# Layer 2 of a two-layer transformer block: four gathers of batch 1 in front of batch 0's root on GpSimd, batch 2's gathers behind batch 1's root, and bounds on three register loads

## The reference

```python
def reference(x, ctx_2048, _lenS2, g_xattn, g_ffn, ...):
    x = x + jnp.tanh(g_xattn[0]) * _L0_xattn_ref(_layernorm(x, axis=-1), ctx_2048, ctx_2048)
    x = x + jnp.tanh(g_ffn[0]) * _L0_ffn_ref(_layernorm(x, axis=-1), L0_ffn_gate_w, L0_ffn_w_gate, L0_ffn_w_up, L0_ffn_w_down)
    x = x + jnp.tanh(g_xattn[1]) * _L1_xattn_ref(_layernorm(x, axis=-1), ctx_2048, _lenS2, L1_xattn_w_q, ...)
    x = x + jnp.tanh(g_ffn[1]) * _L1_ffn_ref(_layernorm(x, axis=-1), L1_ffn_weight, L1_ffn_bias)
    return x
```

```python
    y = jnp.einsum('eci,eih->ech', jax.nn.silu(g) * u, w_down).reshape(E * C, H)
    out = jnp.zeros((T + 1, H), x.dtype).at[t_slot].add(w_slot[:, None] * y)
```

## Time and profile before

| | us |
|---|---|
| median of 3 runs | 1558.16 |
| lowest, highest run | 1550.44, 1563.45 |
| span of the profiled execution, first to last instruction | 1525.3 |
| TensorE busy (matmul) | 1309.4 (86%) |
| VectorE, ScalarE, GpSimd busy | 972.8, 920.1, 520.1 |

### The profile page before, as it was taken

The page is one execution under the profiler, slowest core; times in us unless marked ns, Lnnn a source line. Parts: engine busy times, 40 slices in busy tenths (PEclk is TensorE's granted clock), DMA queues, the critical chain, the costliest instruction groups (busy, mean ns, idle before and its releaser), DMA issues.

```text
span 1525.3 us, 37150 instructions
## 1 busy us (share of the span) xinstructions
PE 1309.4 (86%) x10733; PEld 834.6 (55%) x10734; DVE 972.8 (64%) x2387; ACT 920.1 (60%) x2261; POOL 520.1 (34%) x531
## 2 busy tenths in 40 slices
PE   5888888837999999999999999477989889898984
PEld 3656655524556666665666666144556555555552
DVE  5888888755456665655655633255787777776853
ACT  4777777724556666666666666244766667667661
POOL 1044444455333433332000001665554444541000
PEclk9988888968999999999999999688999999999997
DMA  2044344458888767767676545775654555642000
GB/s 72 29 173 180 146 146 151 156 213 304 269 285 282 256 219 261 238 217 244 218 242 222 181 149 154 126 111 83 98 99 65 104 82 84 100 65 52 15 1 28
DMA packets 96131, 233.39 MB, mean 153 GB/s; under 512 B 11808, under 2 KB 11808, under 8 KB 91424
## 3 DMA queue, kind: packets, MB, share of 16 engines
q0 software_dynamic: 33712, 113.79, 29.8%
q1 hardware_dynamic: 62320, 118.34, 23.3%
HBM read 140.84 MB, written 91.24 MB: 152 GB/s over the span
## 4 chain that ended last, share of the span: by engine, by line
PE 45%; DMA 9%; DVE 9%; issue 8%; ACT 3%; POOL 3%; SPq 1%; DVEq 0%; ACTq 0%; POOLq 0%
PE bank L1305 18%; PE bank L1329 10%; PE bank L1542 6%; DMA xs<-y_tiles,slot_ix 5%; PE bank L1293 4%; PE bank L258 2%; PE bank L1316 1%; PE bank L278 1%; DMA xg<-x_slots 1%; DVE l_nmax L325 1%; PE bank L1548 1%; POOL xs L430 1%; DMA x_slots<-blank 1%; DVE l_stack L379 1%; PE bank L240 1%
## 5 line engine op out<-in xcount | busy, mean ns | idle before, releaser
L1305 PE MATMUL bank<-wh,xT 128*128 x1280 | 343.3, 330 | 4.7 <-DVE hp L1420 4.4
L430 POOL DMA_INDIRECT xs<-y_tiles,slot_ix x120 | 194.6, 1622 | 234.2 <-DMA y_tiles<-ysb 99.1
L293 ACT ACTIVATE l_probs<-bank,l_bias 128x256 f32<-128x256 f32 (+1 forms) x512 | 224.4, 449 | 64.4 <-DVE l_bias L327 64.0
L1305 PE MATMUL bank<-wl,xT 128*128 x640 | 211.4, 330 | 0.0
L325 DVE TENSOR_REDUCE l_nmax<-bank 128x2 f32<-128x512 f32 (+1 forms) x256 | 158.1, 617 | 70.8 <-PE bank L240 41.3
L1410 DVE SCALAR_TENSOR_TENSOR hv<-bank,sg 128x192 f32<-128x192 f32 x160 | 56.9, 356 | 227.5 <-ACT sg L1364 203.5
L1379 ACT ACTIVATE ysb<-bank,xg 128x512 f32<-128x512 f32 x160 | 109.9, 687 | 119.1 <-PE bank L1329 119.1
L305 ACT ACTIVATE l_probsT<-bank 128x512 f32<-128x512 f32 (+1 forms) x256 | 140.0, 547 | 65.6 <-PE bank L278 65.2
L1358 ACT ACTIVATE xT<-bank 128x1024 f16<-128x1024 f16 x160 | 162.5, 1016 | 15.0 <-PE bank L1293 14.8
L1305 PEld LDWEIGHTS bank<-wh,xT 128*128 128x128 f16 x1280 | 126.5, 99 | 81.3 <-issue 11.1
L1329 PE MATMUL bank<-wh,hT 128*128 x480 | 156.1, 380 | 0.9 <-issue 0.9
(11 more groups left out here) (246 smaller groups left out, 2538.1 us busy)
## 6 DMA issues: line engine op xcount, KB each, us to landing
xg<-x_slots SPq DMA_DIRECT2D x160, 272.0 KB, 2.8
y_tiles<-ysb SPq DMA_DIRECT2D x160, 256.0 KB, 2.5
raw<-in_experts_dram POOLq DMA_DIRECT2D x30, 1280.0 KB, 7.1
x_slots<-blank SPq DMA_DIRECT2D x33, 272.0 KB, 3.6
xs<-in_x_dram SPq DMA_DIRECT2D x8, 512.0 KB, 4.4
cbuf<-in_ctx_dram SPq DMA_DIRECT2D x8, 512.0 KB, 5.8
stage<-in_mats_dram POOLq DMA_DIRECT2D x4, 1024.0 KB, 7.8
room<-in_ctx_dram SPq DMA_DIRECT2D x8, 512.0 KB, 4.6
```

Source lines behind the costliest of these rows:

```text
L293: last = self.nc.scalar.activation(self.probs[:, s % 2, u, 0:nk], self.pS[s % 2][:, u * S : u * S + nk], ACT.Exp, bias=self.bias[:, s % 4, ...
L430: return nc.gpsimd.indirect_dma_start(to, None, self.y_tiles[0 : (MT + 1 - k) * P, :], ix, compute_op=ALU.add)
L1305: last = nc.tensor.matmul(bGU[t.place % 2][:, 0:GU], xT[:, t.place % 2, xo + c * P : xo + (c + 1) * P], wp[:, bass.ds(w, 1), c * GU : (c + ...
```

## The change

GpSimd's order at the beginning of `layer1` is altered, and three register loads get bounds.

1. Four of batch 1's 16 gathers stand before batch 0's "xc", four before "P1", four before "P3" and the last four behind it (before: 0, 4, 4, 8).
2. In batch 0's 16 steps, batch 2's gathers stand as 0 in steps 0 to 5, 2 in each of steps 6 to 11, and 1 in each of 12 to 15 (before: 1 in each). Batch 1's "xc" belongs to step 5. Later batches keep one a step.
3. `value_load` of TensorE (L1335) and of VectorE (L1441, L1449) gets `min_val` and `max_val`; this adds instructions that compare the loaded value.

```diff
             def step(t):
-                code = pe.value_load(t_pe[0:1, t.column()])
+                code = pe.value_load(t_pe[0:1, t.column()], min_val=0, max_val=E * E)
...
             for t in range(3):
-                e = dve.value_load(t_e[0:1, t : t + 1])
+                e = dve.value_load(t_e[0:1, t : t + 1], min_val=0, max_val=E - 1)
...
             def step(t):
-                code = dve.value_load(t_dve[0:1, t.column()])
+                code = dve.value_load(t_dve[0:1, t.column()], min_val=0, max_val=2**24)
...
             added = [ROWS]
+            FIRST_ADDS = [0] * 6 + [2] * 6 + [1] * 4
...
-            before = {"P1": 4, "xc": 0, "P3": 4}
+            before = {"xc": 4, "P1": 4, "P3": 4}
             for piece in BEGIN1["pool"]:
                 add_next(before[piece])
                 pool_prep(pool, b0, piece)
...
                     if b.n + 2 < B:
                         pool.wait_ge(at.probs_made, STEPS * b.n + s + 1)
-                        add_next(1)
+                        add_next(1 if b.n else FIRST_ADDS[s])
```

## The result

The changed kernel takes 1575.17 us (median of 4 runs, 1570.7 to 1578.87), the kernel before 1555.67 on the same chip (4 runs, 1550.44 to 1563.45): 1.0123 times as long, 95% interval 1.0093 to 1.0154. It is slower by 19.5 us. I had forecast 1566.5, 8.3 us slower. The measured time lies 0.17 us above the upper end of the range (1555 to 1575). The result is outside the 1% where I had put 0.88.

The account below looks back on a forecast made before the run. The prediction took TensorE to bound the experts and steady layer 2, and GpSimd's gathers the start of layer 2. It summed 1558.16 + 4.5 (layer 2) + 3.9 (VectorE's bounds) to 1566.5 us, range 1555 to 1575.

Parts of the forecast that it names:

- The bottleneck and its move: Layer 2's start: gathers hold batch 1's root 8.31 us; the wait moves to its second RMS root, then batch 2's root.
- Rival (a): Layer 2's gathers: landings follow each other faster without softmax steps between, so the doubling fits; 1551.2 us, chance 0.12.
- Part one, P3 +2.9 us: Batch 0's second RMS root: 12 gathers before it instead of 8, so L1666 and all behind it 2.9 us later.
- Part two, +4.5 us: Batch 2's gathers waiting for step 6: batch 2's root 4.5 us later, kept to the end, at 5.5 us a pair.
- My upper bound, 6.2 a pair: Layer 2's term with 6.2 us for two gathers, at batch 1's second RMS root and batch 2: +10.8 us.
- Part three, VectorE +3.9 us: Experts' stage: bounds on VectorE's load cost 0.25 us at half of 31 weight-split waits, +3.9 us.
- half of the 31: Experts' stage: of 31 `wl` waits for issue, half taken to pay 0.25 us; all would be 7.8 us.
- Part three, TensorE 0 us: Experts' stage: TensorE's queue hides its bounded load, done 2.1 us before the transposes behind it start; no cost.
- rival (c): Experts' stage: bounds show on TensorE too, 0.1 to 0.25 us a tile, 16 to 40 us; 1579 to 1602, chance 0.08.
- 33 us around the span: Whole kernel: the median of the runs, 1558.16 us, about 33 us above the profiled span of 1525.3; outside the change.
- the case: The main forecast: layer 2 +4.5 us, VectorE's bounds +3.9, TensorE's hidden; 1566.5 us, chance 0.80.

Follow-up runs that it names:

- e2: The changed kernel itself, run again on a faster chip; 1538.0 us against 1521.21 for the kernel before.
- m2: The changed kernel with its three bounds taken away and bitwise ANDs on VectorE's values instead, so the move alone; 1568.34 us.
- e1: The kernel before with the change's three bounded loads and nothing moved; 1530.82 us against 1521.21.
- m1: The kernel before, old order, plain loads, with bitwise ANDs on VectorE's values added; 1557.78 us, ratio 1.0024.
- m3: m1 with the first part of the move alone (four gathers before batch 0's root), batch 2's gathers one a step; 1549.28 us.
- n3: The kernel before with bounds on VectorE's loads only, TensorE's load plain; 1524.08 us against 1520.82.
- n4: n3 with a second check of VectorE's value in every tile, two more instructions behind each load; 1533.86 us against 1520.82.
- n2: m1 with the second part of the move alone (batch 2's gathers 0, 2, then 1 a step); 1529.16 us against 1520.82.
- o1: m2 with five of the ten gathers between batch 1's root and P4 put behind P4; 1534.6 us against 1522.39 for the kernel before.
- group m: The runs m1 to m4, timed on one chip, where the kernel before takes 1555.5 us.

## Why the prediction was right and wrong

**The bottleneck and its move: right.** The view of the earlier trace rows and the reading that a wait of 8.31 us would turn into one of P4 and then one of batch 2's root held in the profile after and in e2 and m2. Rival (a), faster landings, is refuted: P4 waits 12.49 us. The Trainium skill's figure for one DMA of this path (DMA: Bandwidth & Descriptors, section "Anatomy of one DMA — SWDGE (gpsimd) path"), an estimated 2.6 us for 256 KB, stands against 4.76 to 5.24 in the chain above; the trace doesn't agree with it here either.

**Part one, P3 +2.9 us: right in size, and read too narrowly.** L1666 of batch 0 is 3.9 us later in the profile after, 2.3 in e2 against e1 and in m2 against m1, 1.6 in m3 against m1. But I weighed the four early gathers only at P3, where they cost. Their worth is at batch 1's root, nine gathers further on, and alone they make the kernel 8.5 us faster (m3). I never worked out the halves of the change by themselves, and so missed that the second takes away what the first had won.

**Part two, +4.5 us: the term was mis-sized; it is 10.6 us (m2 against m1).** Against the forecast's marks, in us from the last transpose of before at 948.4 (rows of the profile after, whose last transpose is at 982.8): first doubled gather 94.2 forecast, 96.5 measured; from it to L1666 of batch 1 26.7 against 28.3; from there to batch 2's `xn` 30.1 against 32.2. That is 6.0 us in all, 3.7 of it pitch. The other 2.3 lie ahead of the first doubled gather and are not the pitch's; in e2, where it stands at 94.8, they are 0.6. The pitch of a half was 5.87 us in the ten gathers (1081.21 to 1104.70 in four) and 5.84 behind P4 (1108.24 to 1137.46 in five), where I took 5.5 out of one row pair and rounded down from 5.57. Nine pitches make each 0.1 us nearly a whole microsecond. My upper bound, 6.2 a pair, gave +10.8, and the result lies there, though the pitch was 5.85. The row that would have told me was in the table of landings: a median of 5.0 plus the 0.8 us that each issue needed in between is 5.8.

**Part three, VectorE +3.9 us: right, in part by luck.** n3 gives 3.5 us (interval 1.1 to 5.9), `wl` waited 0.22 us more for each of 31 splits where I had 0.25. The luck is in the "half of the 31", which no row gave: n4's second pair costs 9.8 us with 6.5 us more of `wl`, and the same rule would have given it less than the first.

**Part three, TensorE 0 us: probably the step that failed.** I wrote that its queue hides the load, from one tile whose transposes started 2.1 us after the load's end. In the profile before, from the end of L1335's load to the next transpose in the array, the median tile has 1.6 us and one in ten under 0.7; in the changed kernel, counted from the end of the SEQ_ASSERT behind the load, the median is 0.65, and 39 of 159 tiles have under 0.5 (8 before). So the tile that I showed was among the best covered third. By two pairs of ratios this costs about 6 us, 0.04 a tile, of the kind that I had put into rival (c) with 0.1 a tile and more; by the medians of the one pair that ran together it is 1.2. The loss of cover is shown; that the array pays these microseconds is argued, since no row shows it waiting for them.

**The sum.** 10.6 for the move, 3.5 for VectorE's bounds and about 6 for TensorE's make 20 us; measured 19.5. Forecast 4.5 + 3.9 + 0 = 8.4. That the time still came within 0.2 us of the range's upper end is in part luck: that end was made of 10.8 for the move, which came, and of 7.8 for VectorE's bounds, of which 3.5 came, and TensorE's share, which the case had at nothing, filled the gap. The "33 us around the span" were an error of reading, too: the profile after has a span of 1568.9 in a run of 1570.7, so 1.8 us lie around it, and the rest was the difference of two kinds of chips. It did not touch the forecast, since no part of the change was priced by it.

## What to carry to other kernels

Where a queue of equal transfers has to pass before several roots, count them up to each root and look for stretches in which the issuing engine idles: here moving transfers behind a root won that root, and the time in which the engine then stood idle came back almost whole at a later one (n2, m2, o1). Work out each half of a change by itself before their sum; here one half was the gain and the other more than its loss. And a pitch that goes into a sum nine times is read from a median plus the issue gap, a cover from the distribution over all tiles; one tile's row stands for neither.

## What the runs showed of the hardware

**Chips of two kinds, 2% apart, in one stage.** The kernel before takes 1521 to 1522 us on three chips and 1555.5 to 1555.7 in the result and in the group m. In every profile of the slower kind the experts begin at 376.8 to 379.5 us, in the faster kind's (the profile before among them) at 343.3 to 346.6; behind that, stage and rest are alike. The same stretch of the same code, 100 to 200 us, in the changed kernel on the chip of the result (busy us by engine, granted clock, DMA share, GB/s):

```profile
100.00:200.00 100.00, 74.12 (x702) 54.48 (x702) 75.00 (x209) 64.31 (x215) 43.97 (x44) 0.83 0.40 151
```

and on a faster one (e2):

```profile
100.00:200.00 100.00, 81.84 (x824) 61.20 (x826) 86.69 (x246) 73.62 (x247) 47.98 (x48) 0.86 0.43 159
```

Some 15% fewer instructions of TensorE and VectorE, at nearly the same clock. The changed kernel's profile has waits put down to "remote" ahead of the experts, e2's has none:

```profile
ACT l_probsT L305 <- remote: 11.8, 8, 2.8
```

What this is stays open; it is why ratios from one chip were compared here and never spans.

**A profile's rest wanders by a few microseconds with the clock.** m3 is 8.5 us faster than m1 by medians and 7.8 ahead at batch 2's `xn`, yet from the last transpose to the end their two profiles agree (575.9). In layer 2's full stretches (us, TensorE's busy time, granted clock, DMA share, GB/s) m3 has

```profile
1067.00:1174.00 107.00, 97.91 (x845) 0.97 0.59 94
1174.00:1238.00 64.00, 57.64 (x479) 0.97 0.51 83
```

and m1

```profile
1180.00:1240.00 60.00, 53.65 (x464) 1.00 0.53 87
1240.00:1302.00 62.00, 55.92 (x469) 0.97 0.53 87
```

m3's profile has four such stretches at 0.97 (also 1360 to 1423 and 1423 to 1485), 296 us together, and m1's has one of 62 us among its six from 1079 to 1487. At 3% of a stretch's length, an estimate that holds where TensorE is full, the 234 us more cost m3 about 7 us, which is about what it had been ahead. Which stretch gets one differs between the executions.
